# Learning-rate exponentials as powers on GpSimd, and a new order around them, in a two-layer fast-weight and attention kernel

## The reference

```
qkv = silu(x @ W_qkv)                      # q, k normalized by their norm
lr  = softplus(x @ W_lr + b_lr + c)        # 3 rates per head and row
for each of 8 chunks of 64 rows:
    gate, hb = k @ w0, k @ w2
    hidden = silu(gate) * hb
    dhidden = v @ w1.T;  dhbm, dgba = its backward through silu and product
    w1g = newtonschulz5((hidden * lr1).T @ v)
    w0g = newtonschulz5((k * lr0).T @ dgba)
    w2g = newtonschulz5((k * lr2).T @ dhbm)
    w0, w1, w2 = column norms of w + wg brought back to their start
    out = silu(q @ w0) * (q @ w2) @ w1
```

## Time and profile before

| What | us |
| --- | --- |
| median of 3 runs | 1005.22 |
| lowest, highest run | 1001.09, 1006.02 |
| profiled execution, its own time | 1001.45 |
| its span | 999.6 |
| busy in the span: PE, DVE, ACT, POOL | 958.0, 690.0, 573.2, 465.4 |

### The profile page before, as it was taken

One profiled execution on the slowest core, in us unless ns is written; L12 is line 12 of the kernel. 1 busy time (PEld: TensorE's weight loads), 2 busy tenths in 40 slices (PEclk: granted clock), 3 DMA queues, 4 the chain that ended last, 5 costly groups with the idle time before them and its releaser, 6 DMA issues.

```text
span 999.6 us, 24780 instructions
## 1 busy us (share of the span) xinstructions
PE 958.0 (96%) x9554; PEld 722.3 (72%) x9554; DVE 690.0 (69%) x2061; ACT 573.2 (57%) x1534; POOL 465.4 (47%) x425
## 2 busy tenths in 40 slices
PE   9799999999999999999999899999999999999987
PEld 7668788788787656574647678786878696868646
DVE  5998898998999822314132776867686668676874
ACT  4677888888888732213132575656565655655541
POOL 1837134033354601001103675866677667779720
PEclk9999999999999999999999999999999999999999
DMA  9221100000000005600004231322232213211202
GB/s 312 80 81 80 43 0 0 0 0 0 1 2 2 2 1 144 245 1 1 0 1 97 51 64 45 75 54 57 49 71 61 54 45 74 64 34 44 96 2 86
DMA packets 32811, 52.94 MB, mean 53 GB/s; under 512 B 7760, under 2 KB 17744, under 8 KB 31824
## 3 DMA queue, kind: packets, MB, share of 16 engines
q1 hardware_dynamic: 32720, 51.69, 18.7%
HBM read 22.57 MB, written 2.10 MB: 25 GB/s over the span
## 4 chain that ended last, share of the span: by engine, by line
PE 47%; DVE 7%; ACT 3%; issue 2%; POOL 1%; DMA 1%; SPq 0%; DVEq 0%; POOLq 0%
PE quad L2218 9%; PE quad L2177 8%; PE quad L1807 8%; PE quad L2121 6%; PE quad L2237 5%; PE quad L2251 4%; DVE act_probs L2576 2%; ACT act_probs L2474 1%; PE quad L2315 1%; DVE wq_wo L2591 1%; DVE x_pairs L2608 1%; PE quad L2185 1%; PE quad L1694 1%; PE quad L2140 1%; ACT hT L1707 1%
## 5 line engine op out<-in xcount | busy, mean ns | idle before, releaser
L2830 POOL TENSOR_TENSOR act_probs<-act_probs,rden 128x512 f32<-128x512 f32 (+3 forms) x128 | 170.2, 1336 | 105.4 <-DVE rden L2596 105.4
L2474 ACT ACTIVATE act_probs<-act_probs,neg_max 128x256 f32<-128x256 f32 (+3 forms) x256 | 141.1, 553 | 84.0 <-DVE neg_max L2576 83.6
L2177 PEld LDWEIGHTS quad<-hT,ug_queries 128*128 128x128 f32 x1024 | 122.6, 192 | 14.3 <-issue 7.7
L2177 PE MATMUL quad<-hT,ug_queries 128*128 128x128 f32 x1024 | 124.7, 275 | 1.1 <-DVE act_probs L1822 0.5
L1807 PE MATMUL quad<-hT,ug_raw_switch 128*128 128x512 f32 x256 | 113.9, 595 | 0.0
L1822 DVE SCALAR_TENSOR_TENSOR act_probs<-quad,ws_up,silu_keys 128x512 f32<-128x512 f32 x32 | 24.0, 750 | 98.2 <-ACT silu_keys L1817 98.2
L1817 ACT ACTIVATE silu_keys<-quad,ws_gate 128x512 f32<-128x512 f32 x32 | 22.0, 687 | 118.6 <-PE quad L1807 118.6
L1807 PEld LDWEIGHTS quad<-hT,ug_raw_switch 128*128 128x128 f32 x256 | 47.5, 190 | 55.0 <-issue 54.8
L2218 PE MATMUL quad<-down_raw_out,ug_raw_switch 128*128 128x256 f32 (+3 forms) x256 | 79.6, 439 | 4.6 <-DVE neg_max L2576 4.6
L2218 PE MATMUL quad<-silu_keys,ug_raw_switch 128*128 128x256 f32 (+3 forms) x256 | 79.5, 439 | 4.0 <-DVE neg_max L2576 2.6
L2596 DVE RECIPROCAL rden<-den 128x2 f32<-128x2 f32 x128 | 20.3, 158 | 87.4 <-ACT act_probs L2474 87.3
(11 more groups left out here) (352 smaller groups left out, 2378.2 us busy)
## 6 DMA issues: line engine op xcount, KB each, us to landing
rope_swapped<-gate SPq DMA_DIRECT2D x120, 64.0 KB, 2.0
ug_raw_switch<-gate SPq DMA_DIRECT2D x60, 128.0 KB, 2.4
ug_raw_switch<-in_wmod SPq DMA_DIRECT2D x4, 512.0 KB, 10.6
x_pairs<-in_x SPq DMA_DIRECT2D x4, 512.0 KB, 7.9
x_rows<-x_pairs SPq DMA_DIRECT2D x8, 256.0 KB, 5.0
wq_wo<-in_wq_nopeT SPq DMA_DIRECT2D x1, 2048.0 KB, 8.5
wq_wo<-in_wo SPq DMA_DIRECT2D x1, 2048.0 KB, 13.1
ug_queries<-in_switch_w SPq DMA_DIRECT2D x1, 2048.0 KB, 7.8
```

The source lines that it names most:

```text
L2177: mm = nc.tensor.matmul(out[:, P * i:P * i + P], w[:, kt, HP * half + i, :], in_order(k.hT[:, kt, b, cols], i), start=(kt == 0), stop=(kt ...
L2474: nc.scalar.activation(tile, tile, ACT.Exp, bias=neg_max[:, r, e:e + 1], scale=-1.0, accum_out=den[:, r, e:e + 1])\
L2830: nc.gpsimd.tensor_tensor(tile, tile, rden[:, t % RING, :].unsqueeze(2).to_broadcast([P, 2, cols]), ALU.mult)\
```

## The change

The exponential of both parts moves from ACT to POOL, as a power of the constant e: a new tile `euler` of one column holds e, and v = euler ** u. With it go ACT's loads of the Exp table and the loads back.

For part 1 the ratio moves too. `ratio_by_root` on POOL adds 2, takes the power of -0.5 and squares it. Together with the series it now stands ahead of POOL's `step(1)`, where before the series alone stood behind that step's `hidden`.

For part 0, PE projects the rates ahead of the first values and not behind them, and DVE runs `start` ahead of the norms of the first q and k. PE's projection of chunk 1's first q and k pair moves from ahead of step 0's gates to behind them. In step 0 ACT squares three states and DVE three, as in the other steps.

```diff
--- before.py
+++ after.py
@@ -42,7 +42,7 @@
 LATE = ((1, 3), (0,), (2,))
 PLACE = (0, 1, 3, 2)
 N_FFN = 16 * 9
-N_CONSTS = 5
+N_CONSTS = 6
 
 
 def to_bf16(v):
@@ -93,6 +93,7 @@
     k.gate_pairs = k.early[:, 0:PAIRS * D].rearrange("p (i d) -> p i d", i=PAIRS)
     k.gates = [k.sbuf(f"gate{g}", [P, B, D]) for g in range(3)]
     k.neg_half, k.half = k.sbuf("neg_half", [P, 4]), k.sbuf("half", [P, PAIRS * 4])
+    k.euler = k.sbuf("euler", [P, 1])
     k.wq_switch, k.w_vo = k.sbuf("ug_raw_switch", [P, 2 * KT * INTER]), k.sbuf("down_raw_out", [P, MT * D])
     k.had, k.su_ug, k.su_dp = k.early[:, L:L + P], k.sbuf("su_ug", [P, KT]), k.sbuf("su_dp", [P, MT])
     k.ws_up, k.ws_gate, k.ws_dp = k.sbuf("ws_up", [P, MT]), k.sbuf("ws_gate", [P, MT]), k.early[:, L + P:L + P + D]
@@ -384,10 +385,20 @@
         at = (slice(0, self.SPLIT), slice(self.SPLIT, NT * self.R))[part]
         return (x[:, at] for x in (self.z, self.u, self.v, self.m, self.k.lr[:].rearrange("p t i r -> p (t i r)")))
 
-    def exponential(self, act, part):
+    def exponential(self, pool, part):
         z, u, v, m, lr = self.columns(part)
-        act.wait_ge(self.step, self.OPS * part + 2)
-        self.k.nc.scalar.activation(v, u, ACT.Exp).then_inc(self.lr_act, 1)
+        pool.wait_ge(self.step, self.OPS * part + 2)
+        self.k.nc.gpsimd.tensor_tensor(v, self.k.euler[:].to_broadcast([P, u.shape[1]]), u, ALU.pow).then_inc(self.lr_act, 1)
+
+    def ratio_by_root(self, pool, part):
+        z, u, v, m, lr = self.columns(part)
+        n = self.OPS * part + 2
+        pool.wait_ge(self.lr_act, part + 1)
+        self.k.nc.gpsimd.tensor_scalar(u, v, 2.0, None, ALU.add).then_inc(self.step, 1)
+        pool.wait_ge(self.step, n + 1)
+        self.k.nc.gpsimd.tensor_tensor(u, u, self.k.neg_half[:, 0:1].to_broadcast([P, u.shape[1]]), ALU.pow).then_inc(self.step, 1)
+        pool.wait_ge(self.step, n + 2)
+        self.k.nc.gpsimd.tensor_tensor(u, u, u, ALU.mult).then_inc(self.step, 1)
 
     def start(self, dve, part):
         nc, R, n = self.k.nc, self.R, self.OPS * part
@@ -412,7 +423,7 @@
 
     def finish(self, eng, by, part, fused):
         z, u, v, m, lr = self.columns(part)
-        n = [self.OPS * part + 4]
+        n = [self.OPS * part + (4 if fused else 5)]
 
         def done(op):
             n[0] += 1
@@ -452,7 +463,7 @@
     G, GT, A, AA, Y, A1, AA1, YT, X2, WN = range(PH)
     ca_b2 = NS_C * NS_A / (NS_B * NS_B)
     QK_BANK = (5, 2)
-    SQUARED, SQUARED_FIRST = (4, 5, 3), (4, 5)
+    SQUARED = (4, 5, 3)
     POLY_ACT = (4, 5, 3)
     A1_DVE = (1,)
     QK_LATE = 0
@@ -710,6 +721,7 @@
                         begin(q, G)
                 gates(t)
                 if first:
+                    project_qk(1, 0)
                     first_norm.turn(pe, 1, 0, bank[NORM_PLACES[0]])
                     pe.wait_ge(rates.step, 1)
                     first_norm.turn(pe, 1, 1, bank[NORM_PLACES[1]])
@@ -919,14 +931,13 @@
             first_norm.wait_halves(pe, 1, 1)
             project_qk(0, 0)
             project_qk(0, 1)
-            project_v(0)
             first_norm.wait_halves(pe, 2, 2)
             rates.project_first(pe)
+            project_v(0)
             pe.wait_ge(s["qkv_acted"], 3)
             turn_v(0, 0)
             turn_qk(0, 0, 1)
             turn_qk(0, 1, 3)
-            project_qk(1, 0)
             step(0, first=True)
             pe.wait_ge(mods.taken, 11)
             with pe.Fori(1, NCH - 2) as t:
@@ -1107,12 +1118,12 @@
                 def root_state(j):
                     g = slice(3 * U * j, 3 * U * j + 3 * U)
                     if j == 1:
-                        act.wait_ge(s["w_squared"], 3 * t + 2)
-                    if first or j == 0:
-                        act.wait_ge(s["w_reduced"], 1 if j == 1 else 3 * t + 4)
+                        act.wait_ge(s["w_squared"], 3 * t + 3)
+                    else:
+                        act.wait_ge(s["w_reduced"], 3 * t + 3)
                     nc.scalar.activation(w_n[:, g], w_rows[:, g], ACT.Sqrt).then_inc(s["w_rooted"], 1)
 
-                for q in SQUARED_FIRST if first else SQUARED:
+                for q in SQUARED:
                     square_state(q)
                 root_state(1)
                 if first:
@@ -1122,9 +1133,6 @@
                 if not more:
                     for f in (5, 6):
                         ffn.take_fold(act, f, bank[FOLD_BANK[f]])
-                if first:
-                    rates.exponential(act, 1)
-                    load_table(ACT.Sqrt)
                 root_state(0)
                 if first:
                     mods.take_rows(act, 1)
@@ -1164,12 +1172,9 @@
             for i in range(PAIRS):
                 silu_qk(0, i)
             silu_v(0)
-            load_table(ACT.Exp)
             take_v(0, 0)
             take_qk(0, 0, 1)
-            rates.exponential(act, 0)
             take_qk(0, 1, 3)
-            load_table(ACT.Silu)
             step(0, first=True)
             with act.Fori(1, NCH - 1) as t:
                 step(t)
@@ -1390,8 +1395,6 @@
 
                 for n, q in enumerate(NQ):
                     update(q)
-                    if first and n == 3:
-                        reduce_state(3)
                 for q in (2, 0, 1):
                     reduce_state(q)
                 factors(1)
@@ -1426,16 +1429,15 @@
             for i in range(PAIRS):
                 dve.wait_ge(s["qkv_acted"], i + 1)
                 square_qk(0, i, (0, 1, 2, 3))
+            rates.start(dve, 0)
             for i in range(PAIRS):
                 norm_first(i)
                 scale_first(i)
-            rates.start(dve, 0)
             first_norm.normalize(dve, nc.vector, 1)
             rates.ratio(dve, 0)
             rates.finish(dve, nc.vector, 0, True)
             step(0, first=True)
             mods.take_turned(dve, 1)
-            rates.ratio(dve, 1)
             with dve.Fori(1, NCH - 1) as t:
                 step(t)
             step(NCH - 1, more=False)
@@ -1511,8 +1513,6 @@
                     pool.wait_ge(rates.step, rates.OPS)
                     rate_rows(0, kl2, 2, 2 * H)
                 hidden(t)
-                if isinstance(t, int) and t == 1:
-                    rates.finish(pool, nc.gpsimd, 1, False)
                 if first:
                     rate_rows(0, kl0, 2, 0)
                     rate_rows(0, vl1, 4, H)
@@ -1543,6 +1543,7 @@
             nc.gpsimd.memset(k.neg_half[:], -0.5).then_inc(k.consts_set, 1)
             rates.pad(pool)
             nc.gpsimd.memset(k.half[:], 0.5).then_inc(k.consts_set, 1)
+            nc.gpsimd.memset(k.euler[:], float(np.e)).then_inc(k.consts_set, 1)
             nc.gpsimd.memset(k.ones[:], 1.0).then_inc(k.consts_set, 1)
             nc.gpsimd.memset(k.ones_bf[:], 1.0).then_inc(k.consts_set, 1)
             pool.wait_ge(k.consts_set, N_CONSTS)
@@ -1550,6 +1551,7 @@
             for i in range(PAIRS):
                 pool.wait_ge(s["first_squared"], i + 1)
                 nc.gpsimd.tensor_tensor(n_qk[:, 4 * i:4 * i + 4], ss_qk[:, 4 * i:4 * i + 4], k.half[:, 0:4], ALU.pow).then_inc(s["first_rooted"], 1)
+            rates.exponential(pool, 0)
             first_norm.root(pool, 1)
             step(0, first=True)
             pool.wait_ge(s["h_copied"], 1)
@@ -1557,6 +1559,9 @@
             pool.wait_ge(mods.step, 5)
             nc.gpsimd.memset(mark[:], 0.0).then_inc(s["out_added"], 1)
             first_norm.wait_halves(pool, 5, 5)
+            rates.exponential(pool, 1)
+            rates.ratio_by_root(pool, 1)
+            rates.finish(pool, nc.gpsimd, 1, False)
             step(1)
             pool.wait_ge(s["h_copied"], 2)
             mods.guard_gates(pool, 1)
```

## The result

| What | before | after |
| --- | --- | --- |
| median of 4 runs, us | 1004.99 | 1021.91 |
| lowest, highest | 1001.09, 1006.02 | 1021.26, 1024.4 |
| profiled execution, own time | 1001.45 | 1024.4 |
| its span | 999.6 | 1022.5 |

The account below looks back on a forecast made before the run. PE was busy 96% of the span, with DVE setting chunk 0's pace. Terms 3.5 + 0 + 13.2 - 0.3 + 1.5 = +17.9 us gave 1019.4 on the profile, 1023.1 on the median; forecast 1022, range 1010 to 1031.

Parts of the forecast that it names:

- the queue on POOL: Chunk 0 on POOL: the power stands behind the second n_qk, 19.72 to 23.8, the norm's root behind it to 24.8.
- the late normalize: Chunk 0 on DVE: normalize waits for POOL's root and moves from 21.12 to 24.85, 3.7 us later.
- the wait for hidden: Step 1: PE's gradient waits for POOL's hidden products, queued behind part 1's powers and series; +13.2 us.
- The price of a power: POOL: 0.41 us plus 0.152 us a column, so 4.06 us for 24 columns and 11.35 us for 72.
- (a): POOL: slope flattens for long rows, a power costs about 1.1 us, nothing stalls; +0.6 us; chance 0.11.
- (b): POOL: half the slope for long rows, 2.2 and 5.9 us a power, no long stall; about +4 us; chance 0.09.
- Part 0: Chunk 0's rates: the power on POOL delays DVE's normalize and backward by 3.7 us, less 0.2; +3.5 us.
- The gates' earlier start: Chunk 0: gates start at 23.1 instead of 23.48, which saves DVE waits inside backward; counted as -0.2 us.
- The end of the step: End of chunk 0's step: removing ACT's exponential and two table loads is hidden behind PE; 0, bounds 0 and -2.6 us.
- the 0.3 us that DVE and ACT were to catch up: Step 1: during PE's wait DVE and ACT catch up on two of six gradient squares; -0.3 us.
- The clock: Behind PE's stall in step 1: work may run at 1.2 GHz, half speed; +1.5 us, bounds 0 and 5.72.
- Rival (c): Faster: the step's end loads (2.6) and the gates' 0.4 us come out at the end; at best -3 us; chance 0.02.

Follow-up runs that it names:

- e_before1: The kernel before, unedited, profiled again as a control for the clock's dip in step 0; 1003.46 us.
- e_sizes: Changed kernel plus ten powers and two multiplies of several sizes and operands at its very end on POOL; only their own durations are read.
- e_root_first: Changed kernel with POOL's root of the first norm's group 1 ahead of part 0's power instead of behind it; 1020.92 us, ratio 1.018.
- e_p0_old: Changed kernel with part 0 wholly as before (old order, exponential on ACT), part 1 as changed; 1016.88 us, ratio 1.0149.
- e_warm: Changed kernel with PE's step 1 written out and 14 unused 128x512 matmuls added in PE's wait for hidden; 1019.93 us, ratio 1.0176.
- e_unroll: Changed kernel with PE's step 1 only written out, no matmuls added; 1019.83 us, ratio 1.0167.
- e_mult: Changed kernel with the three powers of the rates made multiplies of the same shape, so the rates are wrong; 1003.15 us, ratio 1.0003.
- e_best: Changed kernel with part 0 as before; of part 1 only the exponential on POOL, ratio on DVE, series behind hidden; 1002.42 us, ratio 0.9986.
- e_ratio_dve: Changed kernel with part 1's ratio back on DVE, so one 72-column power less on POOL; 1009.81 us, ratio 1.0078.
- e_between: Changed kernel with step 1's hidden products between part 1's two powers on POOL, second power and series behind them; 1017.59 us, ratio 1.0131.

## Why the prediction was right, step by step

The forecast was +17.9 us on the profile; after against e_before1 it is +20.0 at E (327.11 - 307.09), and +20.9 in the executions' own times (1024.4 - 1003.46). The runs' ratio says +19.1, with 15.9 to 22.3 for its interval. The steps of the forecast came as told: the queue on POOL, the late normalize, the wait for hidden and the clock behind it.

- **The price of a power: right, somewhat low.** Forecast 4.06 and 11.35 us. Measured 4.57 and 11.87 in the kernel (13 and 5% more), 4.17 and 11.85 alone (3 and 4% more). Rivals (a) and (b), a flatter slope for long rows, fall with e_sizes: the slope is the same up to 128 columns. The 24-column power has 0.4 us more where it lies at 20 us; it took 4.19 in e_root_first, where it began 1.2 us later. The 0.4 us belong to the place and not to the power (see the root and the multiply there); what causes them stays open.
- **Part 0: right; its term 3.5 was a little small.** Against e_before1 normalize and backward are both 4.09 us later (25.67 - 21.58, 29.68 - 25.59). The term had 3.7 for this; the difference is the 0.4 us that the first instruction on POOL takes more in that place. At U 3.75 us are left, and 3.76 against e_p0_old. That is good to about half a us only, since the dip falls differently in each execution: traces with the same part 0 as after have U from 64.87 (e_warm) to 65.91 (e_unroll). The gates' earlier start did not show as a gain before U for certain: e_mult, which has it, has U at 61.58, against 61.66 and 61.90 in the two profiles.
- **The end of the step: 0, right.** U to the first weights is 11.90 us in both, and e_best, with part 0 as before, confirms that the loads' removal gives nothing. The rows price a load at 1.28 us again.
- **The wait for hidden: right.** Forecast 13.2 less 0.3. With the clock held up (e_warm) part 1 costs 259.21 - 245.43 = 13.8 us. The two powers were 2 x 0.5 = 1.0 us longer than the forecast had them, and 12.9 + 1.0 = 13.9. That this fits so well is partly luck: the series took 7.5 us and not the 8.37 of the earlier trace rows (in e_warm it lies between 90.26 and 97.74), and the 0.3 us that DVE and ACT were to catch up do not show. In e_warm the gradient ends 13.76 us later behind U than before, and E lies 13.78 later.
- **The clock: right, 1.6 us for 1.5, and 2.5 in after's own trace.** 260.83 - 259.21 = 1.6 in e_unroll, and the other four traces with this part 1 agree to about 0.1 us; 261.70 - 259.21 = 2.5 in after. In between lies how long the 0.50 lasts once PE is back: from 99.16 to about 105 us in after, from 95.37 to about 99.7 in e_p0_old, from 99.75 to about 103.4 in e_unroll. Why it differs stays open. The forecast tied the loss to a long stall; e_ratio_dve shows nearly the same loss behind a wait of 2.66 us.
- **Rival (c), faster,** needed room behind the two table loads. There is none (e_best).

Sum by after's trace: 3.75 + 0 + 13.8 + 2.5 = 20.0. That this is E's shift is no proof, since its terms are parts of that shift. The forecast's 17.9 was short by 0.9 in the wait and by 1.0 in the clock; the 0.25 in part 0 is less than that term can be told. With the usual 1.6 us of clock the sum is 19.2, which is what the ratio says.

That the median came out at 1021.91 for a forecast of 1022 is luck. On the profiled execution the forecast was 1019.4 and 1024.4 was measured, 5 us more. Before's profiled execution took 3.5 us less than its median (1004.99) and after's 2.5 us more than its own, and the medians moved by 16.9 us, less than the forecast's own sum. The forecast also had 1019.4 and 1023.1 and gave 1022 without saying why, and its upper end of 1027 goes by 1023.1 (1023.1 - 1.5 + 5.72); from 1022 it is 1026.2.

## What to carry to other kernels

An engine that is half idle is not free: ask, for each window, how long it is, and what stands in its queue behind the new work. One 12 us power cost nothing in an idle window (e_best). A second one, with the series, cost 9.8 us ahead of the scaling of q and k (e_between), and taking it away from ahead of hidden gave 10.7 us (e_ratio_dve against e_unroll). Price an operation by its own rows at two or three sizes, never by a neighbour of the same engine: multiply and power differ here by a factor of 17 at 24 columns. And where a wait is made on TensorE, add the time that it then runs at the lower clock: here 1.6 us behind a wait of 13 us, and nearly as much behind one of 2.66.

## What the runs showed of the hardware

- A power on GpSimd takes 0.159 us for each column of 128 partitions plus 0.4 us, from 8 to 128 columns (e_sizes); at 24 and 72 columns 1, e and -0.5 as base or exponent make no difference. A multiply of 24 columns takes 0.24 us.
- After a wait of 13 us on TensorE the granted clock is 0.50 for about 4 us (e_p0_old) to 6 us (after) of the work behind it, and matmuls of 1.06 us take 2.08. After a wait of 2.66 us (e_ratio_dve) it fell to 0.50 too, about 1 us after PE was back and for some 3.4 us. With matmuls in the wait it stays at 1.00 (e_warm).
- In step 0 the clock fell to 0.50 for 3 to 4 us, between 39 and 50 us, in twelve of the fourteen profiles, two of before's three among them. The one profile of before without it made after look 1 us worse at E than e_before1 does (21.1 against 20.0 us); about half of that is an earlier start.
